# A routed feed-forward stage by dense tiles or by tiles of each expert's own tokens

## The reference

```python
h = _rms(x, w_ln2).reshape(B * S, H)                 # 1024 x 256
logits = h @ w_router                                # 8 experts
probs = jax.nn.softmax(logits, axis=-1)
top_w, top_i = jax.lax.top_k(probs, TOP_K)           # 2 of 8
combine = jnp.sum(jax.nn.one_hot(top_i, N_EXP, dtype=h.dtype) * top_w[..., None], axis=1)
g = jnp.einsum('th,ehi->eti', h, w_gate_e)           # inner width 176
u = jnp.einsum('th,ehi->eti', h, w_up_e)
y = jnp.einsum('eti,eih->eth', jax.nn.silu(g) * u, w_down_e)
routed = jnp.einsum('eth,te->th', y, combine)
sh = jax.nn.silu(h @ w_sh_gate) * (h @ w_sh_up) @ w_sh_down   # inner width 704
sh = sh * jax.nn.sigmoid(h @ w_sh_eg)
x = x + (routed + sh).reshape(B, S, H)
```

## Time and profile before

| | us |
|---|---|
| median of three runs | 2636.81 |
| the profiled execution | 2635.1, its span 2633.0 |
| TensorE busy in the span | 2078.7 |
| VectorE, ScalarE, GpSimd busy | 1525.1, 1180.3, 1044.7 |
| mean granted TensorE clock | 0.857 of full speed |
| first pass of `routed_ffn`, first instruction to the next stage's first | 814.16 to 989.88 |
| second pass, to the first instruction of the end | 2453.72 to 2627.84 |
| the two passes of `moe` | 62 to 257.6 and 359 to 555 |

### The profile page before, as it was taken

How to read it: one execution, slowest core, us unless ns; L and a number is a source line. 1 busy time by engine, 2 the same in 40 slices (tenths; PEclk the granted TensorE clock), 3 DMA queues, 4 the chain that set the end, 5 groups by cost and what they waited for, 6 DMA issues and landing times. The chain is left out here.

```text
span 2633.0 us, 45240 instructions
## 1 busy us (share of the span) xinstructions
PE 2078.7 (79%) x16876; PEld 1605.9 (61%) x16888; DVE 1525.1 (58%) x3266; ACT 1180.3 (45%) x2905; POOL 1044.7 (40%) x965
## 2 busy tenths in 40 slices
PE   8497438978887995967798577976789676779798
PEld 5365225646565874756587466865668665546686
DVE  2222642236675335787876876868778678357432
ACT  3211421126364333853566545655556555236433
POOL 0222012220002542586535864368623767100254
PEclk9698768989998997967799588996789777989799
DMA  8422013210003303321322213222122221120430
GB/s 288 132 24 48 9 39 71 25 44 2 23 2 97 142 0 70 106 73 33 113 80 78 69 50 100 89 63 81 57 89 81 67 69 65 37 55 2 126 113 16
DMA packets 138317, 179.47 MB, mean 68 GB/s; under 512 B 62048, under 2 KB 114544, under 8 KB 132992
## 3 DMA queue, kind: packets, MB, share of 16 engines
q1 hardware_dynamic: 129952, 166.46, 20.4%
q0 software_dynamic: 8160, 10.26, 2.5%
HBM read 154.52 MB, written 22.17 MB: 67 GB/s over the span
## 5 line engine op out<-in xcount | busy, mean ns | idle before, releaser
L2695 DVE SCALAR_TENSOR_TENSOR XT<-M_delta,CW_delta,XT 128x256 f32<-128x256 f32 x576 | 249.0, 495 | 67.7 <-ACT M_delta L2475 39.7
L2146 PE MATMUL PS<-XP_delta,X 128*128 128x268 f32 (+1 forms) x1024 | 247.2, 395 | 19.8 <-DMA X<-in_L_attn_b_heads 15.6
L2146 PEld LDWEIGHTS PS<-XP_delta,X 128*128 128x128 f32 x1024 | 196.0, 193 | 71.8 <-DMA X<-in_L_attn_b_heads 19.8
L1541 PE MATMUL PS<-XP_rffn,UW_rffn 128*128 128x512 f32 x816 | 195.3, 396 | 4.6 <-POOL UW_rffn L1495 4.6
L1541 PEld LDWEIGHTS PS<-XP_rffn,UW_rffn 128*128 128x128 f32 x816 | 156.4, 192 | 38.4 <-issue 5.4
L1273 ACT ACTIVATE PR_attn<-PS,NM_attn 128x256 f32<-128x256 f32 (+1 forms) x384 | 130.8, 448 | 103.5 <-DVE NM_attn L1343 103.5
L1495 POOL TENSOR_TENSOR UW_rffn<-W_rffn,UW_rffn 128x512 fp32r<-128x512 f32 x34 | 43.7, 1286 | 301.5 <-ACT UW_rffn L1602 301.5
L561 POOL DMA_INDIRECT sums<-XS_moe,token_moe x46 | 71.7, 1559 | 221.4 <-ACT XS_moe L661 207.0
L2613 ACT ACTIVATE S_delta<-S_delta,AO_delta 128x128 f32<-128x128 f32 x512 | 159.5, 393 | 0.0
L1663 DVE TENSOR_TENSOR SU_rffn<-PS,CB_rffn 128x512 f32<-128x512 f32 x68 | 47.0, 691 | 179.4 <-PE PS L1541 157.0
L2177 PE MATMUL PS<-KQ_delta,TR_delta 128*128 128x64 f32 x1024 | 133.8, 275 | 9.6 <-ACT TR_delta L2540 8.4
(11 more groups left out here) (459 smaller groups left out, 5259.5 us busy)
## 6 DMA issues: line engine op xcount, KB each, us to landing
M_delta<-gram_delta SPq DMA_DIRECT2D x32, 1280.0 KB, 6.0
X<-in_L_attn_b_heads SPq DMA_DIRECT2D x64, 512.0 KB, 3.5
EW<-in_L_ffn_w SPq DMA_DIRECT2D x24, 512.0 KB, 10.0
CB_rffn<-routes_rffn SPq DMA_DIRECT2D x20, 512.0 KB, 21.9
XN<-in_L_attn_b_outs SPq DMA_DIRECT2D x16, 512.0 KB, 3.7
F_delta<-in_L_attn_b_outs SPq DMA_DIRECT2D x4, 2048.0 KB, 9.5
W_rffn<-in_L_ffn_tiles SPq DMA_DIRECT2D x4, 1536.0 KB, 11.5
slots<-pad SPq DMA_DIRECT2D x2, 2967.0 KB, 14.1
```

Of the source, the lines that this page charges most:

```text
L1541: last = nc.tensor.matmul(PS[:, 4 + 2 * n + q, :], UW[qw][:, r, (q * KD + k) * P:(q * KD + k + 1) * P], XP[qx][:, k, n * NB:(n + 1) * NB], ...
L2146: last = nc.tensor.matmul(PS[:, 1 + i, 0:B * (WIN - halo)], WH[:, r, i, k, :], XP[:, k, :, n * BT + halo:n * BT + WIN], start=(k == 0), st ...
L2695: nc.vector.scalar_tensor_tensor(TMP[:, r, i], RAW[:, r, i, :, tau:tau + BT], CW[:, i, h, tau:tau + 1], TMP[:, r, i], ALU.mult, ALU.add).t ...
```

## The change

`routed_ffn` no longer computes the experts densely. Only the shared expert stays in the split form, now six tiles of 128 hidden units (704 padded to 768) whose split weights are kept for both halves of the tokens. The experts follow the plan of `moe`, with differences. The rows of the normalized tokens are stored in DRAM once; a new class `Routing` computes on TensorE and VectorE, for each of the 23 x 128 slots, which token it holds; GpSimd gathers the rows of each tile by that table (23 indexed transfers); the eight experts' weights (5 MB) lie in SBUF in full float. A tile has gate and up in one product of 352 columns, hidden rows of 176, two turns of 88, and a down product of 256 columns. The answers are stored in order of slots (23 stores by SyncE), and when all are there GpSimd fetches them by slot, 16 indexed transfers, two for each 128 tokens; VectorE multiplies each by its weight and adds it to X. The gate of the shared expert is multiplied in at the end.

TensorE's order: first half of the shared expert with the routing between its tiles, the 23 owners into registers, the 23 expert tiles, then the second half of the shared expert, while the answers come back. The copies of routing weights over the partitions, their DRAM scratch and the loops of tiles (`Fori`) are gone; all is unrolled. Outside the function, `kernel` packs the weights in two arrays, one for the shared expert and one for the eight, and the core has semaphores `gathered` and `returned` which count on over both passes. `Routing.constants`, `choose`, `place` and `owners` are as the like steps in `moe` and left out below; `place` also finds the slot's tile and its lane in it, and `entries` makes from them, for each pair of token and expert, a row of 23 numbers with the token's number at its tile; `table` sums these rows over lanes. Declarations and removed lines are left out too.

```diff
+        self.gathered = [ctx.enter_context(nc.semaphore(f"gathered{t}")) for t in range(SLOTS // P)]
+        self.returned = [ctx.enter_context(nc.semaphore(f"returned{i}")) for i in range(NT)]
+        self.gather_no = self.return_no = 0
...
+    def ranks(self, pe):
+        nc, PS = self.core.nc, self.core.PS
+        pe.wait_ge(self.consts, 2)
+        pe.wait_ge(self.pick_d, 1)
+        m = self.picked[:].rearrange("p i e -> p (i e)")
+        nc.tensor.matmul(PS[:, 6, 0:NT * E], self.ones[:], m, start=True, stop=True).then_inc(self.sum_mm, 1)
+        at = lambda i: PS[:, 7, P + i * E:P + NT * E]
+        nc.tensor.matmul(at(0), self.before[:], m, start=True, stop=False)
+        for i in range(1, NT):
+            last = nc.tensor.matmul(at(i), self.ones[:], m[:, 0:(NT - i) * E], start=False, stop=i == NT - 1)
+        last.then_inc(self.sum_mm, 1)
+    def table(self, pe, spread):
+        nc, PS = self.core.nc, self.core.PS
+        w = (1 + self.weighted) * self.TILES
+        pe.wait_ge(self.entry_d, 1)
+        for j in range(2 * NT):
+            pe.wait_ge(self.spread_d, j // NT + 1)
+            last = nc.tensor.matmul(PS[:, 6, P:P + w], spread[:, j], self.entry[:, j].rearrange("p x t -> p (x t)"),
+                                    start=j == 0, stop=j == 2 * NT - 1)
+        last.then_inc(self.table_mm, 1)
+    def experts(self, pe):
+        pe.wait_ge(self.owner_d, 1)
+        return [pe.value_load(self.owner[0:1, t:t + 1], min_val=0, max_val=E - 1) for t in range(self.TILES)]
...
+    def spread(self, dve, spread, half):
+        nc = self.core.nc
+        h = slice(half * NT, (half + 1) * NT)
+        nc.vector.tensor_tensor(spread[:, h], self.lane[:].unsqueeze(1).broadcast_to([P, NT, P]),
+                                self.lo[:, h].unsqueeze(2).broadcast_to([P, NT, P]), ALU.is_equal).then_inc(self.spread_d, 1)
...
+    def tokens(self, dve, c):
+        nc, PS, t = self.core.nc, self.core.PS, self.TILES
+        dve.wait_ge(self.table_mm, 1)
+        if self.weighted:
+            nc.vector.tensor_copy(self.share[:], PS[:, 6, P + t:P + 2 * t])
+        c.then(nc.vector.tensor_tensor(self.token_f[:], PS[:, 6, P:P + t], self.own[:].broadcast_to([P, t]), ALU.add))
+        nc.vector.tensor_copy(self.token[:], self.token_f[:]).then_inc(self.token_d, 1)
...
+            norm.rows_ready(sp)
+            sp.dma_start(rows.rearrange("(i p) d -> p i d", p=P), G[:, 0]).then_inc(rows_out, 16)
+            sp.dma_start(EWR[:], a["L1_ffn_experts"]).then_inc(experts_in, 16)
+            for t in range(TILES):
+                sp.wait_ge(y_ev, t + 1)
+                sp.dma_start(answers[t * P:(t + 1) * P], XS[:, t]).then_inc(y_out, 16)
...
+            def hidden_low(x):
+                pool.wait_ge(hh_d, x + 1)
+                nc.gpsimd.tensor_tensor(HP[1][:, x % 3], HF[:, x % 2], HP[0][:, x % 3], ALU.subtract).then_inc(hl_d, 1)
+            def gather(t):
+                nc.gpsimd.indirect_dma_start(XS[:, t], None, rows,
+                                             bass.IndirectOffsetOnAxis(ap=token[:, t:t + 1], axis=0)).then_inc(gathered[t], 16)
+            routing.constants(pool)
+            up_low(0)
+            up_low(1)
+            down_low(0)
+            up_low(2)
+            for m in range(ST - 1):
+                hidden_low(m)
+                if m + 1 < ST:
+                    down_low(m + 1)
+                if m + 3 < ST:
+                    up_low(m + 3)
+            pool.wait_ge(rows_out, 16)
+            pool.wait_ge(routing.token_d, 1)
+            for t in range(3):
+                gather(t)
+            hidden_low(ST - 1)
+            for t in range(3, TILES):
+                gather(t)
             nc.gpsimd.tensor_tensor(X[:], X[:], XN[:], ALU.add).then_inc(res_d, 1)
+            pool.wait_ge(routing.slot_d, 1)
+            pool.wait_ge(y_out, 16 * TILES)
+            for i in range(NT):
+                for r in range(2):
+                    nc.gpsimd.indirect_dma_start(
+                        G[:, r, i], None, answers,
+                        bass.IndirectOffsetOnAxis(ap=routing.slot[:, r, i:i + 1], axis=0)).then_inc(returned[i], 16)
...
+            def up(n, m):
+                x = n * ST + m
+                if x == 0:
+                    pe.wait_ge(xl_d, 1)
+                if x == ST:
+                    pe.wait_ge(xl_d, 2)
+                    pe.wait_ge(hr_d, TILES)
+                if x == ST + 1:
+                    pe.wait_ge(ht_d, TILES)
+                if n == 0:
+                    pe.wait_ge(uh_d, m + 1)
+                    pe.wait_ge(ul_d, m + 1)
+                if m >= 2:
+                    pe.wait_ge(h_d, x - 1)
+                for q in range(2):
+                    for k in range(KD):
+                        for step, (qw, qx) in enumerate(PASSES):
+                            last = nc.tensor.matmul(PS[:, 2 + 2 * (m % 2) + q, :],
+                                                    UW[qw][:, m, (q * KD + k) * P:(q * KD + k + 1) * P],
+                                                    XP[qx][:, k, half(n)], start=(k + step == 0),
+                                                    stop=(k == KD - 1 and step == 2))
+                last.then_inc(up_mm, 1)
...
+            def turn(t):
+                pe.wait_ge(gathered[t], here)
+                if t >= 2:
+                    pe.wait_ge(xk_d, t - 1)
+                for k in range(KD):
+                    last = nc.tensor.transpose(PS[:, 6 + t % 2, k * P:(k + 1) * P], XS[:, t, k * P:(k + 1) * P], core.ident[:])
+                last.then_inc(xt_mm, 1)
+            def gate_up(t):
+                pe.wait_ge(xk_d, t + 1)
+                if t >= 2:
+                    pe.wait_ge(hr_d, t - 1)
+                for k in range(KD):
+                    last = nc.tensor.matmul(PS[:, 2 + t % 2, 0:2 * I], XK[:, t % 4, k],
+                                            EWR[:, bass.ds(e[t], 1), k * 2 * I:(k + 1) * 2 * I].rearrange("p o n -> p (o n)"),
+                                            start=(k == 0), stop=(k == KD - 1))
+                last.then_inc(gu_mm, 1)
+            def turn_hidden(t):
+                pe.wait_ge(hr_d, t + 1)
+                if t >= 2:
+                    pe.wait_ge(ht_d, t - 1)
+                for k in range(2):
+                    last = nc.tensor.transpose(PS[0:HC, 4 + t % 2, k * P:(k + 1) * P], HR[:, t % 2, k * HC:(k + 1) * HC],
+                                               core.ident[:])
+                last.then_inc(th_mm, 1)
+            def answer(t):
+                pe.wait_ge(ht_d, t + 1)
+                if t >= 2:
+                    pe.wait_ge(y_ev, t - 1)
+                for k in range(2):
+                    at = 2 * KD * I + k * D
+                    last = nc.tensor.matmul(PS[:, t % 2, 0:D], HT[:, t % 2, k],
+                                            EWR[0:HC, bass.ds(e[t], 1), at:at + D].rearrange("p o n -> p (o n)"),
+                                            start=(k == 0), stop=(k == 1))
+                last.then_inc(y_mm, 1)
...
+            up(0, 1)
+            up(0, 2)
+            down(0, 0)
+            pe.wait_ge(log_d, 1)
+            routing.ranks(pe)
+            up(0, 3)
+            down(0, 1)
+            up(0, 4)
+            down(0, 2)
+            up(0, 5)
+            routing.table(pe, spread)
+            down(0, 3)
+            down(0, 4)
+            down(0, 5)
+            e = routing.experts(pe)
+            pe.wait_ge(h_d, ST)
+            pe.wait_ge(experts_in, 16)
+            pe.wait_ge(routing.token_d, 1)
+            for t in range(3):
+                turn(t)
+            pe.wait_ge(yt_ev, KD)
+            for t in range(TILES):
+                gate_up(t)
+                if t >= 1:
+                    turn_hidden(t - 1)
+                if t + 3 < TILES:
+                    turn(t + 3)
+                if t >= 2:
+                    answer(t - 2)
+            turn_hidden(TILES - 1)
+            answer(TILES - 2)
+            answer(TILES - 1)
+            up(1, 0)
+            pe.wait_ge(xk_d, TILES)
+            shared_rows(0, 6)
+            up(1, 1)
+            up(1, 2)
+            for m in range(ST):
+                down(1, m)
+                if m + 3 < ST:
+                    up(1, m + 3)
+            pe.wait_ge(h_d, 2 * ST)
+            shared_rows(1, 2)
...
+            for m in range(1, ST):
+                silu(m)
+                if m + 3 < ST:
+                    up_high(m + 3)
+                if m + 1 < ST:
+                    down_high(m + 1)
+                high(m)
+            nc.scalar.copy(XP[0][:, :, half(1)], XT[:, :, half(1)]).then_inc(xh_d, 1)
+            turned_out(0)
+            for t in range(TILES):
+                act.wait_ge(gu_mm, t + 1)
+                if t >= 2:
+                    act.wait_ge(hr_d, t - 1)
+                nc.scalar.activation(SR[:, t % 2], PS[:, 2 + t % 2, 0:I], ACT.Silu).then_inc(sr_d, 1)
+                if t >= 2:
```

(43 more changed lines are left out.)

475 lines of the change are left out of this document (263 added, 212 removed).

## The result

The changed kernel took 2643.35 us (median of 19 runs, 2639.2 to 2651.47), the kernel before 2632.63 us on the same chips (19 runs, 2627.44 to 2641.01): a ratio of 1.0037, 95% interval [1.0029, 1.0046]. The forecast was 2604 us, and its range ended at 2630. The profiled execution spans 2644.2 us (before: 2633.0) at a mean granted clock of 0.847 (0.857).

What follows compares the result with a forecast made beforehand. The stage was taken as bound by TensorE. First pass ends at 972.5 instead of 989.9, saving 17.4 us, the second 15.8, together 33.2; from the 2636.8 us median that gives 2604 us, range 2586 to 2630.

Steps and rivals of the forecast that it cites:

- The head and the first half: First pass, shared expert's first half with routing: first up step starts at 826.1, last down step issued at 866.1.
- the stall of the chain: First half: TensorE waits once for the top-2 chain, 1.8 us; bounds 0 and 5 us.
- The owners: Before the expert tiles: 23 register loads with TensorE otherwise idle, 15.1 us, from 866.1 to 881.2.
- The pace of the gathers and fetches: GpSimd's indexed transfers: one each 1.27 us, taken from the scatter of 128 rows.
- The tile's period: Expert loop: TensorE sets the pace at 2.48 us a tile, 57.0 us for 23 tiles.
- The clock of the loop: Expert loop: full clock after the first 5.7 us at half pace, which cost 2.9 us.
- (a): Second half: fetches decide, at the adding scatter's 1.86 us each; 2617 us, chance 0.20.
- (b): Owner reads: cheaper at 10.7 us, or begun 1 us earlier, 5.4 us a pass; 2593 us, chance 0.12.
- (c): Expert loop: bound by issue or its four-engine chain, 3.2 us a tile; 2637 us, no change, chance 0.08.
- (d): Expert loop: does not get the full clock, 23 tiles take 114 us at 0.50; 2712 us, chance 0.05.
- its own mark: Whole pass: the forecast falls if the pass is not between 150 and 168 us long.
- the second half at 0.233 us a matmul: Shared expert's second half: 108 matmuls in 25.2 us plus transposes 0.9, ending at 968, fetches covered by less than 1 us.

Runs made afterwards that it cites:

- e1: Changed kernel with all 39 indexed transfers of a pass replaced by SyncE's plain ones, routed part left out of the result: 2598.67 us, 0.9879 of the kernel before.
- e5: Changed kernel with owners read in the loop, gathers paced by tiles and fetches spaced by waits in the second half: 2591.26 us, 0.9853 of the kernel before.
- e4: Changed kernel with owners read inside the expert loop and gathers paced one per tile, fetches still dense: 2595.18 us, 0.9877 of the kernel before.
- e3: Changed kernel with owners read inside the expert loop, two tiles ahead, gathers still dense: 2635.03 us, 1.0013 of the kernel before.
- e7: Changed kernel with GpSimd's gathers and fetches as plain loads of fixed rows, routed part left out of the result: 2603.98 us, 0.9908 of the kernel before.
- e8: Changed kernel with each gather fetching 64 rows by index, SyncE loading the other 64 plainly from fixed rows: 2653.23 us, 1.0085 of the kernel before.

## Why the prediction was wrong, step by step

**Right.** The head and the first half (826.1 and 866.1 forecast, 826.3 and 868.0 measured; the stall of the chain was 0.37 + 0.97 us, not 1.8, and the down step waited 1.33 us for GpSimd's low part, as described). The missing 1.9 us are in the two up steps behind the router, 7.7 us at a clock of 0.70 where the forecast has 5.6 at full clock. Two small steps of that sum have no row: the terms for the start add up to 825.9, and nothing is named for the 0.8 us between the low part and the last down step. The owners: 15.3 us from the last down step's issue to the first tile for the 15.1 forecast, TensorE idle for 13.7 of them, with the clock at half afterwards. The pace of the gathers and fetches, 1.25 to 1.30 us for the 1.27 of the earlier trace rows. The tile's period, 2.49 us for 2.48. The clock of the loop, 1.00 where it is undisturbed. So rivals (a), (b), (c) and (d) all fall by their own marks, although the time came out near (c)'s. The forecast falls by its own mark too: the pass is 177.2 us long and not between 150 and 168, and the last fetch is issued by 976.2, 9 us ahead of the last down step's end, not within 2.

**Wrong.** Two steps, with one cause. "Each result is asked for a whole tile later, so I let TensorE set the pace", with the gathers counted as free beside it because they come faster than the tiles; and the second half at 0.233 us a matmul, with the fetches "under its cover". Both took the transfers as a cost of GpSimd alone. The loop took 68.2 us instead of 60.4 (883.3 to 951.5), the second half 33.7 instead of 26.4, the tail 5.7 instead of 4.5; with 2.1 us from the first half these are the 18.4 us between 972.5 and 990.9. The second pass lost more, 185.4 against 163.5 (179.3 less the forecast 15.8). e1 shows the size of the missing term: with plain loads in their place the loop is 9 us and the second half 7.5 and 10.6 us shorter, and the median is 2598.67, 5 us below my forecast, which had no such term. That closeness is in part luck: e1 also lacks the three gathers ahead of the last down step, which the forecast has at 3.8 us a pass, and the forecast counts down from a median of 2636.81, where nineteen runs of the kernel before have 2632.63.

Could have shown it? No row of before has dense indexed transfers beside a working TensorE; the prediction says so of VectorE and makes it rival (a), at a price of 0.6 us a fetch. What it lacked is a case in which the wait grows elsewhere than on the engine that issues. An unpriced overlap of 29 us of back-to-back issues with a loop of four engines deserved a wider range on the slow side. Slower had a chance of 0.08, and only 0.03 of it for an unforeseen wait, in the fetched tail alone.

GpSimd and VectorE hold each other up little: the first gather, beside VectorE's subtraction of two SBUF tiles, took 1.39 us, the dearest fetch 1.245, and the median is 0.95 for both. The Trainium skill (GPSIMD Engine Reference, Key points) names contention between GpSimd and VectorE instructions with two SBUF inputs at the SBUF interfaces that they share. The trace agrees in direction: 0.3 to 0.4 us on a few issues, which is far from the time lost.

## What to carry to other kernels

Don't leave long runs of indexed GpSimd transfers back to back beside a chain in which other engines wait for TensorE: give each a wait on the progress of its consumer, one per tile, even if the data could come sooner; where that can't be had, a short pause after every six already helped (e5). Where a wait's releaser is "remote" and the instruction that it needs ended microseconds before, the message is late, not the work; look for what another engine issues just then. And read values that are needed one by one inside the loop that uses them: 23 register loads cost 15 us ahead of it and nothing within it, once the gathers were paced (e4).

## What was unexpected of the hardware

- Updates of TensorE's semaphores came 7 to 15.5 us late during dense indexed transfers (889.06 to 896.37 in the changed kernel, 880.30 to 895.85 in e3), while VectorE's reached TensorE within 0.1 us where one could be followed (889.49 to 889.55 in e3, 2534.51 to 2534.57 in the changed kernel). In the fourteen dense runs of fetches none that a Silu waited for was late in the first 5.6 us, and all were after 12.8 to 13.8 us, so it is no plain lock; by which path it comes about is open.
- The traces of kernels with indexed transfers every 2.5 us or closer lack 36 to 115 records of semaphore updates within 0.35 us of the instruction, nearly all beside these transfers and also where no engine waits; the traces of before, e1 and e7 lack at most one. Whether the taking of these records has a part in the delay, no run shows.
- In e8 TensorE's register steps took up to 0.70 us instead of 0.15, and their spacing grew from 0.65 to up to 4.2 us; in the changed kernel matmuls of one down step came 0.7 to 1.0 us apart instead of 0.23. Whether it is the same cause is open.
- An indexed transfer costs GpSimd 0.95 us plus a pause of 0.30 for 128 rows, 0.91 plus 0.30 for 64, a plain one 0.55 us.
- With half a microsecond more of pause after every sixth fetch half of the second half's stall went away in the first pass and over two thirds in the second (e4: 32.9 / 35.0; e5: 29.5 / 28.6; plain: 26.2). How long a dense run may be was only bounded: four gathers are nearly harmless, six fetches (8.0 us) leave no late Silu, and in runs of 16 the first late one comes after 8.7 to 13.8 us.
